# Row statistics of 28 of 32 tiles worked out in front of each seam of a two-layer decoder, and table waits at first use

## What is computed

```python
def _layernorm(x, axis=-1, eps=1e-05):
    m = jnp.mean(x, axis=axis, keepdims=True)
    v = jnp.var(x, axis=axis, keepdims=True)
    return (x - m) / jnp.sqrt(v + eps)
...
# layer 0: state-space scan (SSM), cross-attention (16 heads, no projections), mixture of 8 routed + 2 shared experts
# layer 1: retention (8 heads, rotary tables, decay table, gate), cross-attention (projected), mixture of 8 experts, top 2
```

## Time and profile before

| | us |
|---|---|
| three runs: 1277.87, 1283.58, 1282.48; median | 1282.48 |
| the profiled execution's own time | 1278.75 |
| its span | 1277.0 |
| seam 1, SSM to attention 0, opens at | 85.5 |
| seam 2, to FFN 0 | 208.5 |
| seam 3, to retention | 516.1 |
| seam 4, to attention 1 | 874.7 |
| seam 5, to FFN 1 | 1008.1 |

### The profile page before, as it was taken

One profiled execution on the slowest core, in us unless ns is written; L12 is line 12 of the kernel. 1 busy time (PEld: TensorE's weight loads), 2 busy tenths in 40 slices (PEclk: granted clock), 3 DMA queues, 4 the chain that ended last, 5 costly groups with the idle time before them and its releaser, 6 DMA issues. The chain is left out here.

```text
span 1277.0 us, 31999 instructions
## 1 busy us (share of the span) xinstructions
PE 1135.2 (89%) x11702; PEld 959.3 (75%) x11702; DVE 830.1 (65%) x1800; ACT 652.2 (51%) x1171; POOL 611.2 (48%) x627
## 2 busy tenths in 40 slices
PE   6979997999999999399999999987899878999930
PEld 4766666689999877288888888875577778999930
DVE  6868997743222343378888888884689675666742
ACT  5417774425566542166665665653687503566610
POOL 4761325126567474733334444333254326566775
PEclk9999999899999999699999999998999888999975
DMA  7001213202233321100000000000110331233332
GB/s 193 10 2 49 54 49 136 102 17 65 71 77 82 98 71 32 39 2 1 0 0 0 1 0 0 0 1 6 21 19 17 113 109 44 68 79 78 87 108 64
DMA packets 61908, 62.64 MB, mean 49 GB/s; under 512 B 12592, under 2 KB 50864, under 8 KB 61296
## 3 DMA queue, kind: packets, MB, share of 16 engines
q1 hardware_dynamic: 51824, 42.52, 11.2%
q0 software_dynamic: 9088, 18.63, 6.3%
q10 hardware_dynamic: 896, 0.17, 0.1%
HBM read 42.67 MB, written 16.52 MB: 46 GB/s over the span
## 5 line engine op out<-in xcount | busy, mean ns | idle before, releaser
L1623 POOL DMA_INDIRECT f_xn<-f_xn_rows,f_source x156 | 149.0, 955 | 49.4 <-issue 48.2
L1977 PE MATMUL f_bank<-f_xT,f_w_tile 128*128 128x128 f32 x1248 | 167.5, 278 | 0.0
L1988 PE MATMUL f_bank<-f_w_down,f_hidden 128*128 x1248 | 165.1, 276 | 0.0
L1977 PEld LDWEIGHTS f_bank<-f_xT,f_w_tile 128*128 128x128 f32 x1248 | 154.4, 195 | 0.0
L1988 PEld LDWEIGHTS f_bank<-f_w_down,f_hidden 128*128 128x128 f32 x1248 | 152.5, 193 | 0.0
L1634 POOL DMA_INDIRECT f_hot_row<-f_slots_y,f_slots x128 | 123.7, 966 | 38.3 <-issue 38.0
L1050 POOL TENSOR_TENSOR ret_rstd<-ret_var,ret_minus_half 128x8 f32<-128x8 f32 x32 | 52.7, 1647 | 173.8 <-DVE ret_var L1089 173.8
L1879 ACT ACTIVATE f_w_tile<-f_w_up 128x512 f32 x156 | 96.3, 620 | 30.1 <-DVE f_owner L1778 28.3
L885 PEld LDWEIGHTS a_mixed_psum<-a_v_diag,a_probT 128*64 128x64 f32 x2048 | 66.6, 139 | 59.9 <-ACT a_probT L837 43.7
L747 POOL TENSOR_TENSOR X<-X,a_mixed 128x128 f32<-128x128 f32 x64 | 29.2, 456 | 159.2 <-DVE a_mixed L780 155.8
L788 DVE TENSOR_REDUCE a_top<-a_scores 128x16 f32<-128x1024 f32 x64 | 78.3, 1224 | 36.0 <-PE a_scores L870 34.8
(11 more groups left out here) (284 smaller groups left out, 2788.1 us busy)
## 6 DMA issues: line engine op xcount, KB each, us to landing
f_slots_y<-f_y_out SPq DMA_DIRECT2D x76, 128.0 KB, 2.0
a_v_rows<-in_ctx SPq DMA_DIRECT2D x16, 256.0 KB, 4.0
f_xn_rows<-f_xn SPq DMA_DIRECT2D x16, 256.0 KB
f_w_up<-in_f_up SPq DMA_DIRECT2D x1, 2560.0 KB, 10.2
f_w_down<-in_f_down SPq DMA_DIRECT2D x1, 2560.0 KB, 17.7
f_xn<-f_xn_rows,f_source POOLq DMA_INDIRECT x156, 2.6
X<-in_x SPq DMA_DIRECT2D x4, 512.0 KB, 7.6
kv_ctxT<-in_ctxT SPq DMA_DIRECT2D x8, 256.0 KB, 5.9
```

Of the source, the lines that this page charges most:

```text
L1623: pool.indirect_dma_start(out=x_in[:, s % RING, :], out_offset=None, in_=xn_rows[:, :], in_offset=bass.IndirectOffsetOnAxis(ap=source[:, s ...
L1977: last = pe.matmul(bank_h[m % 3][:, j * P:(j + 1) * P], w_tile[m % W_RING][:, j * P:(j + 1) * P], xT[m % 3][:], start=True, stop=True)
L1988: last = pe.matmul(bank_y[m % 2][:, 0:D].unsqueeze(1), hidden[m % 3][:, j, :], w_down[:, bass.ds(expert + E0, 1), j, :], start=(j == 0), s ...
```

## The change

Each stage that has a successor gets a second `RowStatistics`, `coming`, that works on the sums of tiles 0 to 27 (`KNOWN = 28`) before the stage ends: on VectorE the seven instructions, on GpSimd the power of tiles 0 to 7. Behind the seam VectorE forms `shift` of tiles 0 to 7 at once and then the statistics of tiles 28 to 31 (in the FFNs behind the eighth `xn`), GpSimd the two other powers; the memset of -0.5 is done once, in SSM. Retention's tables get two semaphores, cos and sin (`rotary_loaded`) and the other four (`loaded`), and each engine waits at the first instruction that reads one. In FFN 0, the last group takes its gathered rows ahead of the shared product.

```diff
+    KNOWN = 28
...
+    def vector_in_front(self, dve):
+        self.vector(dve, slice(0, self.KNOWN))
+    def gpsimd_in_front(self, pool):
         pool.wait_ge(self.var_ready, 1)
-        for begin, end in zip(self.LOTS, self.LOTS[1:]):
-            self.power(pool, slice(begin, end))
+        self.power(pool, slice(0, FIRST))
+        pool.wait_ge(self.rstd_ready, 1)
+    def vector_rest(self, dve):
+        self.vector(dve, slice(self.KNOWN, TILES))
+    def gpsimd_rest(self, pool):
+        self.power(pool, slice(*self.LOTS[1:3]))
+        pool.wait_ge(self.var_ready, 1)
+        self.power(pool, slice(*self.LOTS[2:4]))
...
@@ SSM, vector @@
+                        last.then_inc(S["row_sums"], 1)
+                        if m == N - 2:
+                            dve.wait_ge(S["row_sums"], N - 1)
+                            coming.vector_in_front(dve)
@@ SSM, gpsimd @@
                 pool.wait_ge(S["z_sin_ready"], N)
+                coming.gpsimd_in_front(pool)
                 for j in range(2):
                     setup.spread_values(pool, j, j)
@@ attention, gpsimd @@
                             add(OTILES * before + t, t % 2)
+                            if OTILES * before + t == coming.KNOWN + 1:
+                                coming.gpsimd_in_front(pool)
@@ attention and retention, vector @@
-                        dve.bn_stats(g.stats[:, m, :], g.X[:, m, :])
+                        dve.bn_stats(g.stats[:, m, :], g.X[:, m, :]).then_inc(S["row_sums"], 1)
+                        if isinstance(m, int) and m == coming.KNOWN:
+                            dve.wait_ge(S["row_sums"], coming.KNOWN)
+                            coming.vector_in_front(dve)
@@ retention @@
+                for dst, src in ((cos, "ret_cos"), (sin, "ret_sin")):
+                    sp.dma_start(dst[:], dram[src]).then_inc(S["rotary_loaded"], 16)
...
-                dve.wait_ge(S["loaded"], 16 * 6)
-                act.wait_ge(S["loaded"], 16 * 6)
-                pe.wait_ge(S["loaded"], 16 * 6)
...
+                        if isinstance(m, int) and m == 0:
+                            dve.wait_ge(S["rotary_loaded"], 16 * 2)
                         src = ps_qk[:].rearrange("p (a e) -> p a e", e=R_KEY)
...
+                        if isinstance(m, int) and m == 0:
+                            dve.wait_ge(S["loaded"], 16 * 4)
                         dve.tensor_tensor(decayed[b][:],
...
+                        if isinstance(m, int) and m == 0:
+                            pe.wait_ge(S["loaded"], 16 * 4)
                         for h in range(H):
...
                 skewed(pool, N, 2, step, UNROLL)
+                coming.gpsimd_in_front(pool)
@@ FFN, vector @@
                 for s in range(TILES):
+                    if s == FIRST:
+                        statistics.vector_rest(dve)
...
+                    if shared and m == GROUPS - 1:
+                        dve.wait_ge(S["xn_added"], GROUPS)
+                        for quarter in range(4):
+                            add_rows(dve, m, quarter)
+                        dve.wait_ge(added[1], GTILES * GROUPS)
+                        shared.vector(dve, m)
+                        dve.wait_ge(shared.y_added, GROUPS)
...
+                        if m == GROUPS - 2:
+                            dve.wait_ge(S["row_sums"], GROUPS - 1)
+                            coming.vector_in_front(dve)
```

More of the change, by code:

```diff
@@ L135, in __init__, with vector @@
         self.steps = 0
-    def vector(self, dve, tiles=slice(0, TILES)):
+    def vector(self, dve, tiles):
         g, st = self.g, self.g.stats[:, tiles, :]
@@ L733, in _ @@
             def _(pool):
-                statistics.gpsimd(pool)
+                statistics.gpsimd_rest(pool)
                 for k in range(setup.early, 2):
@@ L762, in shifts @@
                 def shifts(begin, end):
-                    dve.wait_ge(statistics.rstd_ready, 1 if begin < FIRST else len(statistics.LOTS) - 1)
                     dve.scalar_tensor_tensor(out=shift[:, begin:end], in0=g.mean[:, begin:end], scalar=-1.0,
@@ L1553, in add_rows @@
                 dve.wait_ge(gathered[m], gathered_base[m] + 16 * TOP_K * GTILES)
-                if shared:
+                if shared and m < GROUPS - 1:
                     dve.wait_ge(shared.y_added, m + 1)
@@ L1567, in stores_done @@
                 need(eng, stored[k], 16 * len(range(k, upto, Y_RING)))
-        statistics = RowStatistics(g, name, ctx)
+        statistics, coming = RowStatistics(g, name, ctx), None if spec["last"] else RowStatistics(g, f"{name}_next", ctx)
         with nc.Block() as block:
@@ L1843, in _ @@
                         following.low(dve)
-                    if shared and m >= FIRST_UNITS // 2:
+                    if shared and m == GROUPS - 1:
[5 more added lines that the diff above has]
+                        dve.wait_ge(shared.y_added, GROUPS)
+                    elif shared and m >= FIRST_UNITS // 2:
                         add_shared(m)
-                    if parts == 1 or m >= len(ADDED_AT):
+                    if len(ADDED_AT) <= m < GROUPS - 1 or m == GROUPS - 1 and not shared:
                         for quarter in range(4):
```

60 lines of the change are left out of this document (35 added, 25 removed).

## The result

The changed kernel took 1287.79 us (median of 7 executions, 1285.29 to 1289.74), the kernel before, run beside it, 1280.45 us (median of 7, 1277.87 to 1283.58): a ratio of 1.0059, 95% interval 1.0041 to 1.0078. The forecast was 1281.0 us, no measurable difference, range 1275 to 1287. The result lies above the range, by 0.8 us at the median.

The account below looks back on a forecast made before the run. TensorE, busy 89% of the span, idles nearly only around the seams. Terms +3.3 + 1.8 - 2.35 - 2.9 - 1.45 + 0 = -1.6 us, from the 1282.48 us median, gave about 1281 us, range 1275 to 1287.

Parts of the forecast that it names:

- End of FFN 0 (-2.35): End of FFN 0: eight additions and statistics fit VectorE's idle time ahead of the last shared product, gaining 2.35 us.
- Seam 1 (+3.3): SSM to attention: GpSimd's spreading waits behind statistics and power, so the barrier opens 3.3 us later; nothing gained behind it.
- Tails (+0.9 each): Tails of both attentions: seven statistics instructions delay VectorE's tile 29 by 0.9 us each, 1.8 us for both.
- the clock up to 1.5 us at seam 1: Seam 1: a longer TensorE pause lowers its granted clock, slowing the 32 warm-up transpositions by up to 1.5 us.
- Seams 2 and 5 (0): Seams into the FFNs: table loads, warm-up and w_down bound TensorE, so 0; seam 2 from -0.5 to +0.3 us.
- Seam 3 and retention (-2.9): Start of retention: GpSimd's queue loses a 1.2 us wait and one of three powers, gaining 2.9 us.
- the cold rival: Retention: TensorE waits 9 us, stays at 1.2 GHz for a step, costing 8 us; total +7.9, 1290 us; chance 8%.
- Attention 1 (-1.45): Attention 1, behind seam 4: key buffer cleared 2.86 us earlier, so TensorE's 1.45 us wait for keys goes.
- The level: Whole kernel: the sum of -1.6 us carried from the profiled 1278.75 to the three-run median 1282.48, giving 1281 us.
- The 0.5%: Whole kernel: a measurement tells about 0.5% (6.4 us) from no change, so no measurable difference was forecast, chance 81%.

Follow-up runs that it names:

- the base: Kernel before plus only the change's FFN 0 end order and retention's table waits, all statistics at each stage's own start: 1275.39 us, ratio 0.9970.
- the mended kernel: Changed kernel with early statistics in front of seams 3 and 4 only, and FFN 0's power ahead of the last gathers: 1275.46 us, ratio 0.9956.
- the mended kernel without seam 4: The mended kernel, but attention 1 works out its statistics at its own start as before: 1275.51 us, ratio 0.9965.
- the base with a late memset: The base plus one idle GpSimd wait and one-column memset behind FFN 0's last gather: 1280.63 us, ratio 0.9998.

## Why the prediction was wrong

The sum failed by one cost left out (the late drain), two costs that were too small because the clock was not counted in them, and one gain that did not stay.

**End of FFN 0 (-2.35): right in its place, and the step beside it was missed.** The order gives 2.4 us (base alone). But with the statistics the power of tiles 0 to 7 moved behind the last gathers on GpSimd, and I had asked what that power waits for, not what is queued behind it: the block's drain of 9.0 us. It cost 4.0 us (521.6 expected, 525.6 seen; 3.9 us of FFN 0 back when the power moves), and turned the term to +1.6. The rows were there: the drain of before ran from 494.0 to 510.4, and at the end of the program one of 21.4 us ended at 1276.3, again 9.0 us behind the last gather, and 2.7 us behind SyncE's own drain (1273.6), so that there it was what the kernel's end waited for. I had read engines, and not the sequencers' rows at the block's end. This is the step that failed first, the largest of the misses: the prediction gave the place of the power on GpSimd in FFN 0 no price at all, and it cost 4.0 us.

**Seam 1 (+3.3): mechanism right, a little small.** From the start of z_sin to spreading it was 5.1 us and not 1.9, 3.2 more, and the barrier opened another 0.4 us later behind spreading than before: 3.6 us from the start of z_sin to the opening (11.6 against 8.0). Another 1.3 us came earlier in the stage, with the half clock there (below).

**Tails (+0.9 each): the instructions right, the clock not counted.** The delay was 0.98 us in the profile. I had given the clock up to 1.5 us at seam 1 and nothing in the tails, where the pause in front of tile 30's products grew from 1.15 to 2.12 us; in attention 0 TensorE was then at half clock in five profiles of five, and the stage took 125.3 to 127.9 us in those, 123.0 to 124.5 in the nine others. Moving the seven instructions away took both the pause and the half clock out of attention 0, and putting them into the base brought both. The Trainium skill (TensorE: Matmul & The Clock Gate, "What's actually happening") says activity is what releases the throttle, and the prediction quoted it; I applied it behind one pause and not behind this one. The trace agrees, by 1.90 us for 32 products that took 1.11.

**Seams 2 and 5 (0): right.** The first transposition came 5.1 us behind seam 2 in both kernels, and 6.0 us behind seam 5 where it had been 5.7, each time as the 28 warm-up transpositions or the table loads let it. In FFN 0 the shared experts started 22.0 us behind the seam in both kernels, released by w_down:

```profile
237.74 8.80 PE L1410 MATMUL f_bank<-f_xnT,f_w_up 128*128 128x512 f32 x13 [3.50 <-DMA f_w_down<-in_f_down]
```

**Seam 3 and retention (-2.9): right in the profiles, not seen in the medians.** The first qk addition came 17.0 us behind the seam (17.1 foreseen), the stage was 2.3 us shorter in the first profile and 2.8 in the mean of both; TensorE's 9.3 us pause was followed by half clock for nearly 6 us, where it was 4 before, and from its first transposition (545.00) to the next step's products it took 8.4 us and not 7.6. So the cold rival came true with 0.8 us and not with 8.

**Attention 1 (-1.45): the wait went, the gain did not stay.** In the change the transposition that had waited stood 23.3 us behind the seam and not 23.5; in the mended kernel the tenth transposition stood 38.8 us behind it with seam 4 and without, and the medians are the same. So the term was 0.

**The level.** I carried the sum over to 1282.48 us, the median of three; over seven it was 1280.45. So the miss was larger than the 6.8 us between forecast and median: -1.6 us foreseen, +7.3 measured. The 0.5% that I took for the least difference that can be told was too coarse: the intervals here are some 0.2% to either side, and the unchanged kernel moved by 0.2%.

Counted from these: +3.6 (seam 1), +2.0 (tails), +1.6 (end of FFN 0), -2.8 (retention), 0 (attention 1) are 4.4 us by instructions. The medians differ by 7.3 us, the profiles by 8.4. I put the rest down to TensorE at half clock, in the tail of attention 0 (1.2 to 2.4 us) and in the SSM stage (1.3); that is worked out from the profiles, and no run isolates the part in the SSM stage.

**What stays open.** The half clock near 32 us of the SSM stage: z_sin began at 77.5 us in the profiles without it and at 78.8 to 79.2 with it, 1.3 to 1.7 us later. It was in neither profile of before, nor in the base's, nor in that of the mended kernel without seam 4, and it was in the ten others. It isn't the code of that stage: the base and the base with a late memset run the same SSM program, and the first had not the episode and the second had it. Why it comes with some programs is not shown. The parts add up to more than the whole (6.2 us for seam 1, 6.8 for seams 2 and 5, 5.2 for the memset, each against the base, where the whole change is 12.4 above it); that each of the three carries the episode once is a part of this, and not all. And early statistics at seam 3 shorten retention by 0.8 to 2.4 us against the base's 358.0 in the eight profiles that have them (by 2.1 and 2.2 in the mended kernel with seam 4 and without), yet the medians with (1275.46, 1275.51) and without (1275.39) are the same. In those two profiles SSM and FFN 1 together were 4.0 and 2.4 us longer than the base's. So no median shows that statistics in front of any seam gain anything: all that the mended kernel is faster by, the base is too.

## What to carry to other kernels

Before you move an instruction behind an engine's last work, look at what the block's end puts behind it: on GpSimd with gathers in the block that was a drain of 9 us, free only while another engine still works for 9 us. A gap at a barrier is read from the drain rows of every engine's sequencer, not from the name beside the wait. Work moved in front of a barrier was free here only where its engine was idle and nothing at the barrier hung on that engine; of five seams two had such a place, and even these showed in the profiles alone. And the seams that lay behind warm-up transpositions gave nothing for earlier data, and at seam 4 nothing for fewer transpositions.

## What the runs showed of the hardware

- GpSimd's drain at the end of a block with indirect gathers ended 9.0 to 9.3 us behind its last instruction, whether gathers (9.0), a power 4.6 us after the last gather (9.3; the drain's own row is 9.04) or a memset of 0.1 us (9.1; its row is 9.17) came last. In the blocks of SSM, attention and retention, which have none, it ended within 0.3 us.
- A pause of TensorE of 2.1 us and not 1.2 in the last 12 us of attention 0 went with half clock there in five of five profiles against none of nine.
- Warm-up transpositions left out (24 of 32) came with half clock for 10 us instead of 3: no net change.
- The same kernel, run again, came out 0.2% off its reference with an interval that excludes 1, and its executions fell in two groups, some 1277 us at a mean granted clock of 0.952 and some 1280.5 at 0.947.
